# A three-block decoder on one core: a new start, padded tiles, and six of a group's sixteen B products on GpSimd

## The reference

```python
x = x + _L0_attn_ref(_layernorm(x))             # state-space block (Mamba)
x = x + _L0_xattn_ref(_layernorm(x), ctx, ctx)  # 4 heads with exponential gates (mLSTM)
x = x + _L0_ffn_ref(_layernorm(x))              # graph of 6 attention nodes

# of the first block: u after convolution and silu, dt, B and C from projections of u
dA, dBu = exp(dt[..., None] * A), (dt * u)[..., None] * B
h = dA_t * h + dBu_t          # over the 128 steps, 512 channels x 16 states
y = einsum('lbin,bln->bli', h_seq, C) + u * D
# of the last, for each node c
q, k, v = (ew[c, j] * (nodes[...] @ We + be) for j in range(3))
nodes[c] = act_w[c] * mha(q, k, v, Wq[c], Wk[c], Wv[c], Wo[c]) + q
```

## Time and profile before

| | us |
|---|---|
| median of 3 runs (1226.66 to 1229.77) | 1229.7 |
| span of the profiled execution | 1224.7 |
| VectorE busy | 980.0 (80%) |
| TensorE busy, matmuls | 1102.9 (90%) |
| ScalarE busy | 733.8 (60%) |
| GpSimd busy | 15.2 (1%) |

### The profile page before, as it was taken

The page is one execution under the profiler, slowest core; times in us unless marked ns, Lnnn a source line. Parts: engine busy times, 40 slices in busy tenths (PEclk is TensorE's granted clock), DMA queues, the critical chain, the costliest instruction groups (busy, mean ns, idle before and its releaser), DMA issues.

```text
span 1224.7 us, 27095 instructions
## 1 busy us (share of the span) xinstructions
PE 1102.9 (90%) x11540; PEld 842.8 (69%) x11540; DVE 980.0 (80%) x1219; ACT 733.8 (60%) x1728; POOL 15.2 (1%) x32
## 2 busy tenths in 40 slices
PE   8866779999999998999899989999999988998886
PEld 6743456767777676777677767777777766776775
DVE  2398978799998998999999989999988989635122
ACT  3535442776577665776587657765676656544443
POOL 4000000000000000000000000000000000000000
PEclk9777686999999999999999999999999999999998
DMA  6631523013110412041112201041104120000000
GB/s 203 204 115 58 161 93 120 36 36 106 44 62 11 131 36 70 7 134 36 36 37 82 86 17 61 17 124 45 52 11 131 35 62 1 2 2 10 2 1 10
DMA packets 52791, 76.08 MB, mean 62 GB/s; under 512 B 13696, under 2 KB 37504, under 8 KB 52672
## 3 DMA queue, kind: packets, MB, share of 16 engines
q1 hardware_dynamic: 51968, 73.81, 19.2%
q0 software_dynamic: 704, 0.56, 0.2%
HBM read 62.55 MB, written 10.75 MB: 60 GB/s over the span
## 4 chain that ended last, share of the span: by engine, by line
PE 62%; DVE 10%; ACT 8%; issue 3%; DVEq 0%; ACTq 0%
PE ps L632 7%; PE heads L642 7%; PE ps L710 6%; PE ps L703 5%; PE ps L613 5%; PE heads L663 4%; PE heads L671 4%; PE ps L535 4%; PE ps L502 3%; DVE mx L1171 3%; PE ps L559 2%; PE ps L688 2%; PE heads L688 1%; PE heads L613 1%; PE ps L690 1%
## 5 line engine op out<-in xcount | busy, mean ns | idle before, releaser
L1071 DVE TENSOR_TENSOR_SCAN ring<-dec,ring 128x1024 f32<-128x1024 f32 x128 | 292.0, 2281 | 1.7 <-ACT dec L844 1.2
L844 ACT ACTIVATE dec<-dts,a_neg 128x254 f32<-128x254 f32 x512 | 220.0, 500 | 16.8 <-DVE ring L1071 16.7
L1171 DVE TENSOR_REDUCE mx<-heads 128x16 f32<-128x2048 f32 x48 | 109.7, 2286 | 65.3 <-PE heads L663 64.7
L1080 DVE TENSOR_TENSOR ring<-ring,cs 128x1024 f32<-128x1024 f32 x128 | 156.0, 1218 | 1.9
L1064 DVE TENSOR_TENSOR ring<-dtus,bs 128x1024 f32<-128x1024 f32 x128 | 155.1, 1217 | 2.3 <-PE ps L535 1.8
L917 ACT ACTIVATE pr<-heads 128x512 f32<-128x512 f32 x192 | 99.1, 603 | 41.3 <-PE heads L676 41.3
L535 PE MATMUL ps<-ring,fold 128*32 128x256 f32 x1024 | 88.6, 416 | 26.3 <-DVE ring L1080 26.2
L710 PE MATMUL ps<-aT,wo_f 128*128 128x256 f32 x384 | 94.1, 387 | 8.0 <-DVE aT L1180 8.0
L703 PE MATMUL ps<-node,we_f 128*128 128x256 f32 x384 | 99.2, 403 | 0.0
L632 PE MATMUL ps<-node,wq_f 128*128 128x256 f32 x384 | 94.9, 390 | 3.4 <-ACT node L932 3.4
L642 PE MATMUL heads<-wv_f,node 128*128 128x256 f32 x384 | 94.1, 388 | 0.0
(11 more groups left out here) (183 smaller groups left out, 1753.5 us busy)
## 6 DMA issues: line engine op xcount, KB each, us to landing
dts<-dt_rows SPq DMA_DIRECT2D x31, 512.0 KB, 3.9
dtus<-dt_rows SPq DMA_DIRECT2D x31, 512.0 KB, 5.1
node<-in_w_edgeT SPq DMA_DIRECT2D x18, 256.0 KB, 3.1
bs<-bc_rows SPq DMA_DIRECT2D x32, 128.0 KB, 5.0
cs<-bc_rows SPq DMA_DIRECT2D x32, 128.0 KB, 5.1
dt_rows<-dt SPq DMA_DIRECT2D x32, 128.0 KB, 2.4
dt_rows<-th SPq DMA_DIRECT2D x32, 128.0 KB, 2.5
xin<-in_x SPq DMA_DIRECT2D x8, 256.0 KB, 3.1
```

The source lines that it names most:

```text
L844: last = fn(dec[k % 2][:, blk, :, 1:L], dts[c % 2][:, blk, :].rearrange("p (b t) -> p b t", b=GB)[:, :, 1:L], ACT.Exp, scale=a_neg[:, c, b ...
L1071: v.tensor_tensor_scan(states, dec[k % 2][:].rearrange("p k b t -> p (k b t)"), states, 0.0, ALU.mult, ALU.add).then_inc(sig["state"], 1)
L1080: v.tensor_tensor(states[:], states[:], cs[:, q:q + 1, :].broadcast_to([P, BLKS, T]), ALU.mult).then_inc(sig["outflow"], 1)
L1171: v.tensor_reduce(mx[:].rearrange("p (h s) -> p h s", h=HPC)[:, :, 0:STEPS], heads[:].rearrange("p h (s k) -> p h s k", s=STEPS), AX.X, AL ...
```

## The change

**Six products on GpSimd.** `POOL_FED` lists, for each group, the units whose product with B GpSimd does: none in group 0, units 9, 12 and 15 in group 1, and 0, 4, 7, 9, 12 and 15 in groups 2 to 7, 39 in all. Each waits for the scores of the node whose row maxima stand last ahead of it in the list, then for its inputs and its ring buffer. VectorE leaves these out. A scan, and SP where it reloads `bs` and `dtus`, waits for two counters, VectorE's products and GpSimd's.

```diff
+POOL_FED = ((), (9, 12, 15)) + ((0, 4, 7, 9, 12, 15),) * (NG - 2)
...
+            def feed(i, k):
...
+                if k not in POOL_FED[i]:
+                    return
+                grp, node_c = [(grp, step[2]) for step, grp in ORDER[:ORDER.index((("u", "pfeed", k), i))]
+                               if step[:2] == ("f", "max")][-1]
+                after(pool, "smax_ps", grp, node_c + 1)
+                after(pool, f"dtu_in{c % 2}", i, 16 * (c // 2 + c % 2))
+                after(pool, f"bs_in{q}", i, 16)
+                after(pool, "ysum", i, k - RING + 1)
+                g.tensor_tensor(ring[(i * UNITS + k) % RING][:], dtus[c % 2][:],
+                                bs[:, q:q + 1, :].broadcast_to([P, BLKS, T]), ALU.mult).then_inc(sig["pool_fed"], 1)
...
             def feed(i, k):
...
+                if k in POOL_FED[i]:
+                    return
...
             def scan(i, k):
                 states = ring[(i * UNITS + k) % RING][:].rearrange("p k t -> p (k t)")
                 after(dve, "decay", i, k + 1)
-                after(dve, "inflow", i, k + 1)
+                wait_fed(dve, i, k + 1)
```

```diff
-                            last = mm(MA[:, a * T:(a + 1) * T], wdt[:, m * P:(m + 1) * P], xdn[0:R, :],
+                            last = mm(MA[:, a * T:(a + 1) * T], wdt[:, m * P:(m + 1) * P], xdn[:],
                                       start=True, stop=True)
...
-                    for h in range(XH):
-                        r0, at = h % 2 * XD, h // 2 * T
+                    for a in range(HC):
                         for b in range(GB):
-                            last = mm(ML[i > 0][r0:r0 + XD, at + b * L:at + (b + 1) * L], vaug[:, b, h, 0:XD], ident,
-                                      start=True, stop=True, tile_position=(0, r0))
+                            last = tr(ML[i > 0][:, a * T + b * L:a * T + (b + 1) * L],
+                                      vaug[:, b, a, 1:1 + P], ident)
...
-                        last = mm(ML[i > 0][0:GROWS, 0:T], wgate[:, k, :], src[:, k % HC, :],
+                        last = mm(ML[i > 0][:, 0:T], wgate_all[:, k * GROWS:k * GROWS + P], src[:, k % HC, :],
...
-                    for j, src in enumerate((grow, gtop)):
-                        for b in range(GB):
-                            last = tr(ML[i > 0][:, (j * GB + b) * XH:(j * GB + b + 1) * XH], src[:, b * L:(b + 1) * L],
-                                      cst[0:XH, C_ID:C_ID + XH])
+                    for b in range(GB):
+                        last = tr(ML[i > 0][:, b * P:(b + 1) * P], zeros[:, b * L:(b + 1) * L], ident)
```

```diff
+        IN_BANK = ((MA, ED, MY, MA), (MA,) * 4)
...
-                    else:
+                    elif i:
                         after(pe, "inproj_read", i, j)
+                    elif j == 3:
+                        after(pe, "inproj_read", 0, 1)
...
-                    after(pe, "u_ready", i, 1)
+                    if i == 0:
+                        pe.wait_ge(sig["u_first"], 1)
+                    else:
+                        after(pe, "u_ready", i, 1)
                     for k in range(IC):
+                        if i == 0 and k == 2:
+                            after(pe, "u_ready", i, 1)
```

**The order.** The units' steps are split into four tables by engine (decays; VectorE's; sums; loads), so that they move apart from one another, and all tables have new numbers, in quarters of a step; a line of the old and of the new is enough to see their kind:

```diff
-X_AT = [26, 37, 41, 42, 45, 47, 48, 50, 54, 55, 56, 57, 57, 58, 63, 64]
+    x1=[31.75, 37, 42, 43.25, 46, 47.5, 49, 53, 54.25, 55.25, 56.25, 57, 57, 59, 63.25, 64.5],
+    ug1=[-30.95, -19.95, -8.95, 3.05, 14.05, 25.05],
```

More of the change, by code:

```diff
@@ new lines @@
+SHIFT = dict(
+    a1=[-10, 2, 2, 2.25, 2, 2, 2.25],
+    us1=[16.5, 25.5, 20.25, 28.75, 20.25, 29.25, 15.25],
+    ua1=[0.75, 1, 0.5, 1, 1, 1, 0.5],
+    uv1=[1, 1.25, 1, 1, 1, 1, 1],
+    up1=[1.25, 1, 1, 1.5, 1, 0.75, 0.5],
+    x1=[1, 1, 1, 1, 1.25, 1, 1.25],
+)
+ORDER = [(FSLOTS * g + n, 0, g, n, step) for g in range(NG) for n, step in enumerate(F_STEPS)]
+for _rank, (_name, _steps, _groups) in enumerate((
+        ("a0", A_STEPS, (0,)),
+        ("a1", A_STEPS, range(1, NG)),
+        ("p", P_STEPS, (0,)),
+        ("ua0", DECAY_STEPS, (0,)),
+        ("ua1", DECAY_STEPS, range(1, NG)),
+        ("ug1", [("u", "pfeed", k) for k in POOL_FED[NG - 1]], range(1, NG)),
+        ("up0", SUM_STEPS, (0,)),
+        ("up1", SUM_STEPS, range(1, NG)),
+        ("us0", SPREAD_STEPS, (0,)),
+        ("us1", SPREAD_STEPS, range(1, NG)),
+        ("uv0", UNIT_STEPS, (0,)),
+        ("uv1", UNIT_STEPS, range(1, NG)),
+        ("w", W_STEPS, (0,)),
+        ("x0", X0_STEPS, (0,)),
+        ("x1", X_STEPS, range(1, NG)))):
+    for _k, g in enumerate(_groups):
+        _shift = SHIFT[_name][_k] if _name in SHIFT else 0
+        ORDER += [(FSLOTS * max(g - 1, 0) + at + _shift, 1 + _rank, g, n, step)
+                  for n, (step, at) in enumerate(zip(_steps, AT[_name]))]
@@ L288, in after, with wait_fed @@
                 eng.wait_ge(sig[name], value)
+        def wait_fed(eng, i, n):
+            mine = sum(UNITS - len(POOL_FED[g]) for g in range(i)) + len([k for k in range(n) if k not in POOL_FED[i]])
+            pools = sum(len(POOL_FED[g]) for g in range(i)) + len([k for k in POOL_FED[i] if k < n])
+            if mine:
+                eng.wait_ge(sig["inflow"], mine)
+            if pools:
+                eng.wait_ge(sig["pool_fed"], pools)
         def walk(steps):
@@ L369, in mamba_in @@
                     if i == 0:
-                        for q in range(NGRP):
-                            spread_rows(0, q)
+                        spread_row(0, 0, 0)
                 if step == 10:
@@ L375, in mamba_in @@
                         first_chunk(sp, dts, dt, "dt")
+                        for q in range(NGRP):
+                            for j in range(1 if q == 0 else 0, 2):
+                                spread_row(0, q, j)
                     after(sp, "dt_ready", i, 1)
@@ L400, in chunk @@
                     return
-                for j, (dst, name, used) in enumerate(((dts, "dt", "decay"), (dtus, "dtu", "inflow"))):
+                for j, (dst, name) in enumerate(((dts, "dt"), (dtus, "dtu"))):
                     after(sp, f"{name}_stored", i, 16 * BLKS)
-                    after(sp, used, i, (c - 1) * CUNITS)
+                    if j:
+                        wait_fed(sp, i - (c < 1), (c - 1) * CUNITS if c else UNITS - CUNITS)
+                    else:
+                        after(sp, "decay", i, (c - 1) * CUNITS)
                     sp.dma_start(dst[c % 2][:].rearrange("p k t -> p (k t)"),
@@ L600, in head_values @@
                 for b in range(GB):
-                    last = mm(head_bank(i, h)[:, b * XP:(b + 1) * XP], cT[:, h % 2, b, :], vaug[:, b, h, :], start=True, stop=True)
+                    last = mm(head_bank(i, h)[:, b * XP:(b + 1) * XP], cT[:, h % 2, b, :],
+                              vaug[:, b, h // 2, h % 2 * XP:(h % 2 + 1) * XP], start=True, stop=True)
                 last.then_inc(sig["h_ps"], 1)
@@ L783, in mamba_in @@
                     fn(gate[p][:, 0:2, :].rearrange("p a b -> p (a b)"), MA[:], ACT.Copy).then_inc(sig["inproj_read"], 1)
-                if step == 5:
+                if i and step == 5:
                     after(act, "inproj_ps", i, 4)
@@ L1002, in layer_norm @@
                 last.then_inc(sig[f"ln_var{n}"], 1)
+                if i == 0 and n == 1:
+                    setup()
                 after(dve, f"ln_rstd{n}", i, 1)
@@ L1161, in mlstm_out @@
                     return
+                m_chain.wait(m_chain.n)
                 xi = xr[i % 2]
-                heads_of = xi[:].rearrange("p b (h d) -> p b h d", h=XH)
-                v.tensor_tensor(heads_of, heads_of, hrow[:, :, :, 0:XD], ALU.add).then_inc(sig["x2_ready"], 1)
+                heads_of = xi[:].rearrange("p b (a n) -> p b a n", a=HC)
+                v.tensor_tensor(heads_of, heads_of, hrow[:, :, :, 1:1 + P], ALU.add).then_inc(sig["x2_ready"], 1)
                 after(dve, "x2_ready", i, 1)
```

207 lines of the change are left out of this document (124 added, 83 removed), and 4 rows, old and new, of the table U_AT.

## The result

The changed kernel takes 1270.4 us against 1229.7, a ratio of 1.0335 (95% interval 1.0309 to 1.036): 40.6 us slower, where the prediction had 13 faster. Its profiled execution has a span of 1267.8 us, 43.1 more than before.

What follows compares the result with a forecast made beforehand. It took VectorE as the bound before the first maxima and early in group 6, TensorE in groups 0 to 5. Start -2 and -5, tiles -4, products -2.4 sum to -13.4: span 1211.3, time 1216 us, range 1200 to 1238.

Steps and rivals of the forecast that it cites:

- The likeliest case: Whole kernel: the forecast of 1216 us, taken as 1209 to 1223, chance 0.44.
- the first rival: GpSimd's late products hold VectorE, at node 5's layer norm and a product by C: slower, put at 1238, chance 0.23.
- TensorE's new order at 0: Middle groups: sums move behind queries and out-projection; one wait grows as another shrinks: 0, within 1 us a group.
- SP's transfers at nothing: SP's transfers of B rows and dtu chunks wait for both counters, but for the same units: no cost.
- The start: -7: Up to the first maxima: first scan 2 us sooner, then 5 us less of VectorE's idle time.
- rival (2): Start: nothing gained, x_proj comes later behind the fillers and the bias waits longer: 1223, chance 0.15.
- the -2: Up to the first scan: 2 us sooner (-5 to +3), from earlier convolution, dts' loads and softplus.
- the -5: First scan to first maxima: 5 us less (-9 to 0), as VectorE's idle waits are covered.
- Padded tiles: -0.65 a group: TensorE, groups 0 to 5: fewer, full transposes of context and gates save 0.65 x 6 = 4 us (0 to -5).
- Products on VectorE's side: 0 in groups 0 to 5 and -2.4 in group 6: Moved products gain nothing where TensorE is the bound; products 9 and 12 save 2.4 us in group 6 (0 to -3.7).
- (3): Middle groups: fuller tiles and fewer waits end the stretches at 1.2 GHz, -10 us: 1206, chance 0.13.
- (4): VectorE is the bound of the middle groups after all: 44 us less, 1172, chance 0.05.

Runs made afterwards that it cites:

- g1: The kernel before with only the changed kernel's slots for TensorE's sums (add) of groups 1 to 7: 1247.5 us (1.0156).
- f3: The kernel before with only the changed kernel's slots for SP's spread transfers in groups 1 to 7: 1237.4 us (1.0077).
- g4: The kernel before with only the changed kernel's slots for ScalarE's decays of groups 1 to 7: 1243.7 us (1.0144).
- h1: The kernel before with only units 0, 4, 7, 9, 12 and 15 on GpSimd, as in the changed kernel: 1252.8 us (1.0194).
- i2: The changed kernel with units 0, 4, 6, 8, 11 and 14 on GpSimd instead: 1249.5 us (1.0173).
- e4: The changed kernel with three GpSimd memsets in place of each of its six products: 1246.8 us (1.0153).
- f4: The changed kernel with SP's transfer order of before and three GpSimd memsets in place of each of its six products: 1234.9 us (1.0051).
- g2: The changed kernel, start and padded tiles kept, every engine in the old order from group 2 on, all products on VectorE: 1237.7 us (1.0087).
- i1: The kernel before with units 0, 4, 6, 8, 11 and 14 on GpSimd: 1228.5 us (0.9999).
- e2: The changed kernel with only units 0 and 4 on GpSimd: 1253.3 us (1.021).
- e1: The changed kernel with all sixteen products of a group on VectorE again: 1267.6 us (1.0335).
- run 29: Not a label: the text says "costs the run 29 us"; that run is the kernel before with six products on GpSimd, 1252.8 us (1.0194).

## Why the prediction was wrong, step by step

**The likeliest case fell; the first rival stood in its mechanism and covers about half of the loss.** The mechanism is shown: product 7 begins behind the late sum at 623.55, where the prediction had placed it by the trace of before, and holds the second layer-norm operation. The rival put both its places at 4.5 us a group; six products instead of memsets make 22 us of the changed kernel, 3.7 a group, and the six in the kernel before make its groups 134.4 instead of 130.1, 4.3 more. That the sizes are so near is in part luck: in the changed kernel the layer norm is held in four of groups 0 to 5 and a product with C in two, 2.0 us each time, and in the kernel before neither place is struck in these groups. And without any product on GpSimd the changed kernel is as slow (1.0335), which no rival had. Two more things were wrong with it. It got a chance of 0.23, because no row of before could show GpSimd beside VectorE, although every other part of it stood in the order. And its time was set at 1238, between its two places, instead of at the 1243 that both give. The holding struck more places than the two named: the softplus operation (2.1 us), the gate (0.5 to 1.6), the scan (0.7). The Trainium skill (SBUF — State Buffer, Who interferes with whom) had the rule: two SBUF inputs against a GpSimd instruction that reads SBUF exclude each other, and so does a one-input operation of VectorE in its faster two-port mode. The trace agrees: the softplus, with two inputs, 3.32 instead of 1.20, the layer norm's tensor_scalar, with one, 2.43 instead of 0.41 (in which mode it ran no row shows), and the maxima, a reduction, never longer than 2.29.

**TensorE's new order at 0 failed.** The step said that one wait grows as the other shrinks. Alone (g1) the new places of the sums cost 21 us. I had looked at what TensorE waits for, and not at who waits for the sums: VectorE's products with B, for their buffer (15.3 us), and its gather (6.1), with the maxima behind it in one place.

**SP's transfers at nothing failed.** The step was true of the waits and silent on the queue. SP's chunk 2 had moved behind the output store, which waits for node 5's end. The new slots of all of SP's spread transfers cost 9 us alone (f3), with 14.6 us of waits for chunk 2's rows.

**The decays were missed.** No sentence of the prediction costs ScalarE's decays moving ahead of qT in the middle groups: 17 us alone (g4), by a way that is shown only in part.

These three do not add up with the holding. Six products alone cost 24 us (h1); the change nearly without holding costs 21 (i2 against the kernel before); together 40.6. Within the 21 the pieces overlap: alone they come to 47 us. In the changed kernel itself one piece was measured, with memsets in place of the products: SP's order is 12 of 19 us there, and 6 are left (e4, f4). How those 6, and the loss with all products done, divide among sums, decays, start and the rest of VectorE's order stays open.

**The start: -7, measured +2.1.** The first scan came at 61.47 instead of 59.07, the far side of the bounds. The last input product and node 0's bias now stand ahead of x_proj, which began at 37.09. From the first scan to the first maxima it is 165.6 us, 165.9 before: the idle time that I saw covered came back as other waits for biases of nodes, 3.9 us (I had 1.5 for one) and 5.0 just ahead of the maxima, where the 5.3 that I had left in stood. Since the runs with the old start have their first maxima anywhere from 223.8 to 229.6, and those with the new one from 226.7 to 229.0, the +2.1 itself can't be told from no change; rival (2), no gain, is what holds. Over all runs the two terms part: the first scan comes at 57.9 to 59.1 with the old start and at 60.8 to 64.3 with the new one, so the -2 failed in its sign; from there to the first maxima it is 165.8 to 170.4 us in the kernel before and its runs with other products, and 164.3 to 165.8 with the new start, so a part of the -5 may be there.

**Padded tiles: -0.65 a group.** The old order with padded tiles (g2) has 129.4 us in groups 1 to 5, 130.0 before. That fits, but i1 with the old tiles has 129.2, so it is not settled.

**Products on VectorE's side: 0 in groups 0 to 5 and -2.4 in group 6.** Right in size: with memsets 129.5 instead of 130.1 a group, inside the bounds, and -2.7 in group 6. In the changed kernel group 6 gained 0.4. Its three products held VectorE for 4.2 us there, but i1, in which nothing is held, gained no more, so the reason stays open. GpSimd's price, 2.85 us as the upper bound, is 2.35 where nothing holds it; the Trainium skill's estimate (GPSIMD Engine Reference, Elementwise — side-by-side cycle accounting) was 2.4, and the trace agrees with it better than with the bound I took. Rivals (3) and (4) did not occur: the stretches at 1.2 GHz grew (granted clock 0.96 over groups 0 to 5, 0.98 before), and TensorE is busy 125.2 us in group 2. Yet (4) may have a grain in it: in the new order two products off VectorE pay 14 us (e2 against e1), though the shorter waits ahead of its products could pay them as well.

## What to carry to other kernels

Before moving work to GpSimd, list for each piece when it can really begin, by its last semaphore, and which VectorE instructions run for its whole length from then on; if any of them reads two SBUF operands, or is a tensor_scalar from SBUF to SBUF as the layer norm's here, count the overlap as lost on either engine. A cover must be an instruction that isn't held, as a reduction from PSUM here, and the piece must find its buffer free when the cover begins. And where a table of numbers changes, go through every queue, SP's and ScalarE's too, asking of each step that moved not only what it waits for but who waits for it and for what now stands behind it.

## What the runs showed of the hardware

A product with B on GpSimd and a VectorE operation with two SBUF inputs exclude each other for nearly their whole length, and it goes by issue: a product that begins inside a scan lasts 4.02 us instead of 2.35, and the VectorE instruction behind it lasts 3.32 instead of 1.20. A memset on GpSimd of the same size, 0.952 us, holds nothing and isn't held. VectorE's operations with one operand in PSUM aren't held either: the gather `u<-u,vec,ps` beside a product lasts 0.46 to 0.48 us, as elsewhere, while the two-input gate right behind it is held. What I had not expected is that a held instruction's cost hardly shrinks on its way to the end: in the kernel before the six products make VectorE's instructions 2.12 x 6 + 1.48 x 6 + 0.09 x 96 = 30 us longer by the rows of h1 and its memset run, and the holding costs the run 29 us, though VectorE sat idle for 9.2 us in a middle group before the change and for 94 us between the first and the seventh group's first maxima in both of these runs.
